# Cross-attention and a small mixture of experts on one core: attention by single query tiles, keys loaded transposed, the query and key weights folded

## The reference

```
h  = layernorm(x)                                # x: 4 x 256 x 128
q  = h @ Wq + bq;  k = ctx @ Wk + bk;  v = ctx @ Wv + bv      # ctx: 4 x 1601 x 128
s  = clip(q @ k.T / sqrt(128), -100, 100)
x  = x + softmax(s) @ v
f  = layernorm(x)
p  = softmax(f @ Wr.T + br);  top 2 of 8
gu = f @ GU[e] + b;  gate = min(gu[:256], 7);  up = clip(gu[256:], -7, 7)
y  = ((up + 1) * gate * sigmoid(1.702 * gate)) @ DN[e] + bd
x  = x + sum over the top 2 of p[e] * y[e]
```

## Time and profile before

| | us |
|---|---|
| median of 3 runs (all: 164.24, 164.44, 165.79) | 164.44 |
| the profiled execution, its own time | 165.41 |
| its span in the trace | 163.4 |
| busy: PE / DVE / ACT / POOL | 154.9 / 104.9 / 102.3 / 35.3 |
| first transposes of the normalised x on PE | 6.61 |
| first scores | 12.25 |
| first expert matmuls (`gate_up(0, 0, 0)`) | 68.32 |
| last `project_v` | 82.70 |
| first `down` | 87.40 |

### The profile page before, as it was taken

How to read it: one execution, slowest core, us unless ns; L and a number is a source line. 1 busy time by engine, 2 the same in 40 slices (tenths; PEclk the granted TensorE clock), 3 DMA queues, 4 the chain that set the end, 5 groups by cost and what they waited for, 6 DMA issues and landing times.

```text
span 163.4 us, 2880 instructions
## 1 busy us (share of the span) xinstructions
PE 154.9 (95%) x932; PEld 136.4 (83%) x932; DVE 104.9 (64%) x305; ACT 102.3 (63%) x209; POOL 35.3 (22%) x36
## 2 busy tenths in 40 slices
PE   7789999999999999998999999799999999999993
PEld 7769987889989989886787888688888888887982
DVE  0769997296977487251757399556665566642864
ACT  3069775757464655738755673499777777887550
POOL 1291000000030030010018472143321233333030
PEclk9999999999999999999999999999999999999999
DMA  4999970000000000000000000000000000000022
GB/s 134 251 403 386 382 222 0 0 0 6 0 0 0 0 0 4 0 2 0 4 0 0 0 0 4 0 0 0 2 4 0 0 0 0 0 2 0 0 68 64
DMA packets 5188, 7.92 MB, mean 48 GB/s; under 512 B 300, under 2 KB 3000, under 8 KB 5176
## 3 DMA queue, kind: packets, MB, share of 16 engines
q1 hardware_dynamic: 5032, 7.63, 14.2%
q10 hardware_dynamic: 144, 0.13, 0.3%
HBM read 7.24 MB, written 0.52 MB: 48 GB/s over the span
## 4 chain that ended last, share of the span: by engine, by line
PE 76%; DVE 11%; ACT 6%; POOL 2%; DMA 2%; issue 2%; DVEq 0%
PE T L1087 17%; PE S L881 11%; PE S L883 11%; PE S L882 11%; PE O L966 10%; PE T L954 5%; DVE sc L565 4%; PE T L923 2%; DVE ct_lo L552 2%; POOL rstd L268 2%; DMA x_sb<-in_x 2%; PE S L1087 1%; ACT gate L436 1%; ACT pr L365 1%; ACT pT L373 1%
## 5 line engine op out<-in xcount | busy, mean ns | idle before, releaser
L779 DVE TENSOR_SCALAR up<-up 128x512 f32<-128x512 f32 x32 | 15.0, 468 | 27.6 <-ACT up L442 27.6
L462 ACT ACTIVATE xn<-T,w_scaled 128x128 f32<-128x128 f32 x56 | 16.1, 374 | 19.0 <-PE T L1087 14.0
L966 PE MATMUL O<-pT,ctx_sb 128*128 128x256 f32 (+1 forms) x104 | 26.7, 382 | 1.3 <-ACT pT L373 1.2
L881 PE MATMUL S<-x_hi,w_hi 128*128 128x512 f32 x64 | 26.7, 417 | 1.2 <-ACT gate L436 1.2
L373 ACT ACTIVATE pT<-T 128x512 f32<-128x512 f32 (+1 forms) x28 | 15.5, 568 | 19.0 <-PE T L954 19.0
L305 POOL TENSOR_TENSOR x<-x,xn 128x512 f32<-128x512 f32 x13 | 17.2, 1327 | 38.8 <-ACT xn L462 38.8
L883 PE MATMUL S<-x_hi,w_lo 128*128 128x512 f32 x64 | 25.4, 397 | 0.0
L882 PE MATMUL S<-x_lo,w_hi 128*128 128x512 f32 x64 | 25.2, 395 | 0.0
L436 ACT ACTIVATE gate<-S,gate_bias 128x512 f32<-128x512 f32 x32 | 22.7, 708 | 3.0 <-PE S L883 3.0
L268 POOL TENSOR_TENSOR rstd<-ve,minus_half 128x2 f32<-128x2 f32 (+1 forms) x7 | 7.1, 1010 | 74.2 <-DVE ve L609 68.6
L442 ACT ACTIVATE up<-S,up_bias 128x512 f32<-128x512 f32 x32 | 22.6, 707 | 0.0
(11 more groups left out here) (116 smaller groups left out, 249.3 us busy)
## 6 DMA issues: line engine op xcount, KB each, us to landing
ctx_sb<-in_ctx SPq DMA_DIRECT2D x3, 768.0 KB
gu_sb<-in_gu SPq DMA_DIRECT2D x1, 2048.0 KB, 13.2
ctx_sb<-in_ctx SPq DMA_DIRECT2D x1, 512.0 KB
x_sb<-in_x SPq DMA_DIRECT2D x1, 384.0 KB, 3.8
ctx_sb<-in_ctx SPq DMA_DIRECT2D x1, 256.0 KB, 5.0
out_x<-xn SPq DMA_DIRECT2D x1, 256.0 KB, 2.3
out_x<-xn SPq DMA_DIRECT2D x2, 128.0 KB, 1.8
ctx_sb<-in_ctx SPq DMA_DIRECT2D x4, 32.5 KB
```

Source lines behind the costliest of these rows:

```text
L462: ins = nc.scalar.activation(y_sb[:, k % 2, t * DIM:(t + 1) * DIM], T[k % 2][:, t * DIM:(t + 1) * DIM], ACT.Copy, scale=w_scaled[:, bass.d ...
L881: nc.tensor.matmul(dst, a_hi, b_hi, start=True, stop=False)
L966: ins = nc.tensor.matmul(O[:, 0:TPB * P], ctx_sb[b][0:rows, t, :], pT[0:rows, t, :], start=(t == 0), stop=(t == KT - 1))
```

## The change

Six things change together.

1. The host adds the contexts in a transposed copy (`in_ctxT`); contexts 1 to 3 are loaded from it as well (`keysT_sb`), so only context 0 is still transposed on TensorE. ACT makes the high parts of contexts 1 to 3 from that copy in halves (`keys_hi`), and POOL the low parts in four chunks (`keys_lo`).
2. Wq and Wk are multiplied once at the start (`fold_weights`), scaled and copied by ACT (`copy_fold`), and g is one matmul from the transposed x (`fold_keys`); `project_q` and ACT's `evict_q` go.
3. Probabilities are transposed and summed by single query tiles, in matmuls of 128 columns, tile n behind the scores of tile n + 1.
4. ACT, not SP, issues the load of x tiles 2 to 7, and the other loads stand in another order.
5. The layernorm moments of tiles 5 to 7 move on DVE from the start to behind the second tile's clips.
6. At the handover the Silu table is brought in by an activation of one column between copies, and the first expert's activations come behind all copies of `pT`; the products of batches 0 to 2 with Wv go to bank M; the first two experts' weights are split in the loop.

```diff
 @block.sync
-            sp.dma_start(x_sb[:, TPB:TILES], x_v[:, TPB:TILES]).then_inc(x1_in, 16)
-            for b in range(BATCHES):
...
+            def keys_transposed(b):
+                sp.dma_start(keysT_sb[:, b - 1, :], ctxT_in[b]).then_inc(keysT_in[b - 1], 16)
...
+            keys(0)
+            keys_transposed(1)
...
+            keys(1); keys_transposed(2)
...
+            keys(2); keys_transposed(3); keys(3)
 @block.gpsimd
+            def keys_lo(b, half):
+                pool.wait_ge(keys_hi_ready, (b - 1) * 2 + half + 1)
+                for c in range(half * 2, half * 2 + 2):
+                    c0, _, w = SCORE_CHUNKS[c]
+                    nc.gpsimd.tensor_tensor(ct_lo[b % 2][:, c0:c0 + w], keysT_sb[:, b - 1, c0:c0 + w],
+                                            ct_hi[b % 2][:, c0:c0 + w].bitcast(F32), ALU.subtract).then_inc(keys_lo_ready, 1)
...
+            keys_lo(1, 0); keys_lo(1, 1); keys_lo(2, 0); keys_lo(2, 1); root2(0)
+            keys_lo(3, 0); root2(1); keys_lo(3, 1); root2(2); root2(3)
 @block.scalar
+            act.dma_start(x_sb[:, TPB:TILES], x_v[:, TPB:TILES]).then_inc(x1_in, 16)
...
+            def keys_hi(b, half):
+                c0, w = SCORE_CHUNKS[2 * half][0], sum(w for _, _, w in SCORE_CHUNKS[2 * half:2 * half + 2])
+                act.wait_ge(keysT_in[b - 1], 16)
+                if b >= 2:
+                    act.wait_ge(s_done, (b - 1) * TPB * NCH)
+                nc.scalar.activation(ct_hi[b % 2][:, c0:c0 + w], keysT_sb[:, b - 1, c0:c0 + w],
+                                     ACT.Copy).then_inc(keys_hi_ready, 1)
...
+            copy_fold(); copy_xT(0); split_ctx(0); split_g(0); split_ctx(1); split_ctx(2); split_ctx(3); normalise(1)
+            keys_hi(1, 0); copy_xT(1); exponentials(0); split_g(1); keys_hi(1, 1); copies(0); exponentials(1); normalise(2)
+            keys_hi(2, 0); copies(1); copy_xT(2); exponentials(2); copy_oT(0); split_g(2); keys_hi(2, 1); copies(2)
+            exponentials(3); split_x2(0); copies(3); exponentials(4); copy_oT(1); keys_hi(3, 0); copies(4)
+            exponentials(5); split_x2(1); keys_hi(3, 1); copies(5); exponentials(6); copy_oT(2); copies(6); exponentials(7)
...
+            copy_pT(TILES - 1, 0); copy_pT(TILES - 1, 1)
+            nc.scalar.activation(table_switch[:], minus_half[:, 0:1], ACT.Silu)
+            copy_pT(TILES - 1, 2); copy_pT(TILES - 1, 3)
+            expert(0, 0, 0); copy_oT(last)
 @block.vector
+            moments(x_sb, stats, mv, ve, *PREP[1], var_ready, neg_mean)
...
+            clip_scores(0); finish_scores(0); clip_scores(1); finish_scores(1); split_g(1)
+            moments(x_sb, stats, mv, ve, *PREP[2], var_ready, neg_mean)
+            clip_scores(2); finish_scores(2)
...
 @block.tensor
+            def fold_weights():
+                pe.wait_ge(att_in, 16)
+                nc.tensor.matmul(M[:, 0:DIM], wqT_sb, wkT_sb, start=True, stop=True)
+                nc.tensor.matmul(M[:, DIM:DIM + 1], wqT_sb, bk_sb, start=True, stop=True)
+                nc.tensor.matmul(M[:, DIM + 1:DIM + 2], wkT_sb, bq_sb, start=True, stop=True)
+                nc.tensor.matmul(M[:, DIM + 2:DIM + 3], bq_sb.to_broadcast([P, P]), bk_sb, start=True,
+                                 stop=True).then_inc(fold_done, 1)
...
             def transpose_xn(j):
                 if j == 0:
                     pe.wait_ge(const_ready, 3)
+                    pe.wait_ge(fold_ready, 1)
...
             def scores(n, chunks):
+                    elif n % TPB == 0:
+                        pe.wait_ge(keys_lo_ready, (b - 1) * NCH + c + 1)
...
+            def finish_sum(n):
+                weighted_sum(n, 0)
+                transpose_p(n, 2)
+                transpose_p(n, 3)
+                for g in range(1, len(PT_GROUPS)):
+                    weighted_sum(n, g)
...
+            for n in range(1, TILES - 1):
+                b = (n - 2) // TPB
+                scores(n + 1, [0, 1, 2])
+                if n == 1: transpose_xn(2)
+                if n >= 2 and n % TPB == 0: project_v(b)
+                transpose_p(n, 0)
+                scores(n + 1, [3])
+                if n >= 3 and n % TPB == 1: router(b)
+                transpose_p(n, 1)
+                finish_sum(n)
+                if n == 1: fold_keys(2)
+                if n >= 2 and n % TPB == 0: transpose_x2(b)
```

More of the change, by code:

```diff
@@ L66, with pt_use, build @@
 PAIR_STEPS = [(0, 0), (1, 0), (0, 1), (1, 1)]
[L69 to L86, removed]
+CT_USE = len(CTX_GROUPS) // 2
+PT_USE = len(PT_GROUPS) // 2
+def pt_use(n, g):
+    return g % 2, CT_USE + n * PT_USE + g // 2
+T_TOTAL = [CT_USE + TILES * PT_USE] * 2
+def build(nc, x, ctx_in, ctxT_in, att_w, more_w, rows, gu, dn, db, out):
     es = ExitStack()
@@ L374, in copy_pT, with copies @@
                                      ACT.Copy).then_inc(t_free[bank], 1)
+            def copies(n):
+                for g in range(len(PT_GROUPS)):
+                    copy_pT(n, g)
             def copy_oT(b):
@@ L393, in _ @@
[L393 to L425 removed]
+            keys_hi(1, 0)
@@ new lines, in _ @@
+            copy_xT(1)
+            exponentials(0)
+            split_g(1)
+            keys_hi(1, 1)
+            copies(0)
+            exponentials(1)
+            normalise(2)
+            keys_hi(2, 0)
+            copies(1)
+            copy_xT(2)
+            exponentials(2)
+            copy_oT(0)
+            split_g(2)
+            keys_hi(2, 1)
+            copies(2)
+            exponentials(3)
+            split_x2(0)
+            copies(3)
+            exponentials(4)
+            copy_oT(1)
@@ L426, in _ @@
+            keys_hi(3, 0)
+            copies(4)
+            exponentials(5)
+            split_x2(1)
+            keys_hi(3, 1)
+            copies(5)
+            exponentials(6)
+            copy_oT(2)
+            copies(6)
+            exponentials(7)
             last = BATCHES - 1
@@ L929, in scores @@
+            def scores(n, chunks):
+                b = n // TPB
                 tok = slice(n * P, (n + 1) * P)
@@ new lines, in _ @@
+            transpose_p(0, 1)
+            finish_sum(0)
+            for n in range(1, TILES - 1):
+                b = (n - 2) // TPB
+                scores(n + 1, [0, 1, 2])
+                if n == 1:
+                    transpose_xn(2)
+                if n >= 2 and n % TPB == 0:
+                    project_v(b)
+                transpose_p(n, 0)
+                scores(n + 1, [3])
+                if n >= 3 and n % TPB == 1:
+                    router(b)
+                transpose_p(n, 1)
+                finish_sum(n)
+                if n == 1:
+                    fold_keys(2)
+                if n >= 2 and n % TPB == 0:
+                    transpose_x2(b)
```

456 lines of the change are left out of this document (190 added, 266 removed).

## The result

The changed kernel takes 167.4 us (median of 4: 166.29, 167.28, 167.52, 167.74) against 164.49 for the kernel before. The ratio, taken from the means of 167.2 and 164.8, is 1.0149, 95% interval 1.0078 to 1.022. Run once more beside the experiments it took 166.46, a ratio of 1.0127 (1.0079 to 1.0175). By these ratios it is slower by 1.3 to 1.5%. Some executions of nearly every kernel are 2 to 4 us longer than the rest, of the kernel before also those whose mean granted clock is 0.979, and all medians and ratios in this document leave them out.

What follows compares the result with a forecast made beforehand. TensorE's queue was taken as the bound. From first scores at 12.85, 54.6 us of work and 6.9 of waits give first expert matmuls at 74.4; 14.8 of handover gives down at 89.2, +1.8 on 164.44: 166.2, range 163.0 to 168.4.

Steps and rivals of the forecast that it cites:

- the wait of tile 2 for GpSimd: Scores of tile 2 wait for GpSimd's low parts of context 1: 3.0 us, with two later chunks 4.0 in all.
- Start: Up to the first scores: the fold takes 1.4 us, and the first scores come at 12.85, 0.6 later than before.
- 12.3 to 13.5: Sign of being wrong: the first scores start outside this span, in us.
- X: The first transpose of the normalised x on TensorE: 6.61 before, forecast at 7.5 (7.0 to 8.0), behind the fold's copy.
- Tile 0 and the wait: TensorE ends the sum of tile 0 at X+17.0, then stalls 3.0 us until the first low-part chunk at X+20.0.
- a rival about the clock: At the start, TensorE's clock rises later because of new pauses: 167.1 to 168.2, chance 0.13.
- Tiles 3 to 7: 6.6 us of TensorE per tile; DVE and ACT fit, except waits of 0.35 at project_v(0) and 1.45 for context 3.
- Handover: First expert matmuls at 74.4 to first down at 89.2: 14.8 us, the removed table wait given back to the routing.
- (a): Low parts of context 1 come in time for tile 2; the 4.0 us go, 162.2, faster; chance 0.18.
- (b): At the start the clock stays 1.2 GHz through tile 0's scores, which end 0.9 later; 167.1 to 168.2; chance 0.13.
- (c): DVE holds GpSimd up: chunks of contexts 1 and 3 on the path cost 1.4 us each; 168.2; chance 0.07.
- The queue's 4.5 us: TensorE's queue gets 4.5 shorter: 39 transposes (3.9) and two q projections (1.3) go, narrower passes add 0.7.

Runs made afterwards that it cites:

- before_again: The kernel before, unaltered, run again with a profile: 163.97 us.
- after_again: The changed kernel, unaltered, run again beside the experiments: 166.46 us, ratio to before 1.0127.
- filled_wait: The changed kernel with 13 fp32 matmuls on zeros added behind the sum of tile 0, so TensorE works through its wait: 166.09 us, ratio 1.0079.
- routing_first: The changed kernel with the first half's routing comparisons and weights on DVE ahead of the first up-projection clip: 165.51 us, ratio 1.0091.
- parts_apart: parts_first with one wait added: GpSimd starts context 1's low parts only when DVE has clipped tile 0 from below: 162.03 us, ratio 0.9844.
- filled_transposes: The changed kernel with tile 2's wait filled by 26 transposes of 128x128 on TensorE: 166.14 us, ratio 1.0085.
- xb_behind: The changed kernel with only xb moved on GpSimd, to behind the low parts of context 1: 163.07 us, ratio 0.9916.
- best: parts_apart with context 3's high parts together, its second low part behind DVE's normalising, routing before the first clip, g_lo of tiles 5 to 7 earlier: 158.64 us.
- after: The changed kernel's first measurement and profile, nothing altered: 167.4 us, ratio to before 1.0149.
- context3_early: The changed kernel with context 3's second high part on ACT directly behind the first, ahead of tile 4's copies: 166.53 us, ratio 1.015.
- parts_first: The changed kernel with GpSimd making context 1's low parts before the root for tiles 5 to 7 and before xb: 162.54 us, ratio 0.9865.

## Why the prediction was right

It said slower by 1.8, 166.2, with 163.0 to 168.4 as its range; measured are 167.4 and 166.46. The forecast's main step, the wait of tile 2 for GpSimd, was right in order and size and stood at the right place in the queue, though 1.9 us earlier in time. But two of its terms were wrong with opposite signs, so that the total came out this near is in part luck. Set against `before_again`, whose clock rose as early as the changed kernel's, the first `down` is 3.6 later and the forecast of 1.8 is 1.8 low.

- **Start.** Predicted first scores at 12.85, 0.6 later than before; they came at 10.82, outside the 12.3 to 13.5 that the prediction itself had set as a sign of being wrong. 1.36 of the difference is the clock, which rose early in this execution as in `before_again` (0.20 a warm-up pass where the earlier trace rows had 0.23). The remaining 0.67 is the fold, which I let cost 0.6: its eight passes took 0.95 (4.91 to 5.86) where I had 1.4, and X is 6.64, released by DVE's normalised x and not by the fold (in `after_again` the copy of the fold releases it, at 6.74, so the two are about level). That step was mis-sized by taking one execution's slow start for a property of the kernel.
- **Tile 0 and the wait.** From the first scores to the end of the sum of tile 0: predicted 11.65, measured 11.80. The wait: predicted 3.0, measured 3.04. `xb` took 2.35 for 2.37; a chunk took 1.01 for contexts 1 and 3 and 0.87 for context 2 against my 1.05. The Trainium skill (GPSIMD Engine Reference, "Elementwise — side-by-side cycle accounting"), by which I had made an estimate of 0.88, fits the one and is 0.13 short for the other.
- **What I missed:** that the wait itself would slow TensorE down afterwards. From the scores of tile 2 to the first weighted sum of tile 1 I had 4.5 us, `filled_wait` shows 4.34 and the changed kernel 6.18. I had a rival about the clock, but placed it at the start and for the pauses there; the long pause that my own sum created at 24.5 I did not put to it. This failure and the start cancel to 0.03 at the scores of tile 3.
- **Tiles 3 to 7.** Predicted 37.85 from the scores of tile 3 to the first expert matmuls, measured 38.58: `project_v(0)` waits 0.65 instead of 0.35, context 3's low part 1.25 instead of 1.45, the rest is spread over the tiles.
- **Handover.** Predicted 14.8, measured 14.47; the residual came 10.57 behind the first expert matmuls against 10.85. `routing_first` shows that the clip ahead of the routing costs 1.0 of it. That the table load left the path is read from the rows alone; no run tried it.
- **Rivals.** (a), low parts in time, is what `parts_apart` makes of the kernel: 162.03 where its sum said 162.2; the order of the change excludes it. Its first scores came at 11.39 and not at 12.85, so that agreement is in part luck too. (b), a later rise at the start, did not come in the profiles of the changed kernel, where the rise came earlier instead; it came in the profile of `filled_transposes` and costs 3.6 there against an early rise, 2.3 against the rise at 10.79 from which (b) counted its 0.9 to 2.0. (c), DVE holding GpSimd up, did not come on the path; it exists (1.27 a chunk in `xb_behind`), and so does the reverse, which costs time as soon as GpSimd's work is moved.
- **The queue's 4.5 us.** From the first scores to the first expert matmuls `before_again` takes 56.03 with 0.76 of waits that the timeline shows, 55.3 of work. `best` takes 56.43 (10.71 to 67.14) with 0.78 of waits and one tile more summed, 4.3: 51.4 of work. So 3.9 left the queue where I had 4.5; my sum of work was 1.0 short in both kernels, which I had booked as waits of before.

Still open: why the clock, by the durations, rises before 6.3 us in twelve of the fourteen profiles, near 10.8 in one and at 17.2 in one (that of `filled_transposes`, so the fold does not prevent it); why the slow stretch behind the same idle time is once 6.8 and three times 3.4 long; what lowers the clock in some executions of the kernel before; and why a chunk of context 2 takes 0.87 and one of contexts 1 and 3 takes 1.01.

## What to carry to other kernels

Before work is given to an idle engine that runs in order, write down what already stands in its queue ahead of the new step and when each of those is released; here a root whose input had been moved and one addition of 2.4 us that nobody needed for 15 us made more than the loss: with both behind the low parts the kernel is faster than before. Price a long idle stretch of TensorE with the slow stretch behind it, and look at more than one execution of the kernel before if its first microseconds show slow matmuls. When a step of GpSimd is moved, list the DVE steps from SBUF to SBUF that it will then lie beside.

## What the runs showed of the hardware

- TensorE idle for 3.04 us behind a busy stretch was followed by a granted clock of 0.5 in all four profiles that have it (`after`, `after_again`, `routing_first`, `context3_early`), for 6.8 us once and for 3.4 us three times. Idle for 0.76 at the same place (`xb_behind`), or filled with matmuls or transposes, it stayed at 1.0.
- GpSimd's subtraction of 128x400 in SBUF beside DVE: DVE's clip from below of 1601 columns, from SBUF to SBUF, takes 1.91 instead of 1.04 (`parts_first`), two normalisings of 128 columns 2.05 instead of 0.60 (`context3_early`); in `xb_behind` GpSimd's chunk too takes 1.27 instead of 0.87; clips from PSUM (0.63) and statistics (0.67) take what they always do. The Trainium skill (GPSIMD Engine Reference, section 1, Specifications) says that GpSimd's way to SBUF is shared with VectorE and names as contenders instructions in a 2-port mode or with two SBUF inputs; the slowed steps run from SBUF to SBUF with one tensor each, which fits the first kind, but the trace does not name the mode, and the page has no price.
- Early in the span the granted clock reads 1.00 in every slice, while fp32 passes of 256 columns take 0.45 in one execution and 0.26 in another (`before_again`, 7.50 to 8.01 for two); the durations tell the clock there, the row of granted clocks does not.
